# A negated-mean normalise on GpSimd and an earlier second-half projection in a layernorm, attention and mixture-of-experts kernel

## The reference

```python
xn = (x - mean(x)) / sqrt(var(x) + 1e-5)          # per token, over 128 features

# attention, per sequence of 256 tokens
w = einsum('bsd,btd->bst', xn @ W + b, xn)
w = exp(tanh(w * lw)) * off_diag                   # lw[s, t] = 1 / (|s - t| + 1e-7), 0 on the diagonal
attn = (w / (sum(w) + 1e-7)) @ xn

# mixture of 8 experts, top 2, 176 hidden units each, bf16 products
scores = sigmoid(xn @ gate_w.T)                    # top 2 of scores + expert_bias
routed = sum over the two of  square(relu((xn * score) @ w_up[e].T)) @ w_down[e].T

# shared expert, 176 hidden units, float32
shared = square(relu(xn @ shared_w_up.T)) @ shared_w_down.T

out = x + attn + routed + shared
```

## Time and profile before

| | |
|---|---|
| time, median of 3 runs | 118.33 us (117.22, 118.33 and 118.81) |
| span of the profiled execution, first to last instruction | 116.0 us |
| its own time, as the runs are timed | not given; the span lies 2.3 us below the median |
| busy: TensorE, its weight loads | 110.6 us, 85.1 us |
| busy: VectorE, ScalarE, GpSimd | 101.1 us, 89.5 us, 69.6 us |
| granted TensorE clock, mean of the span | 1.000 |

### The profile page before, as it was taken

One profiled execution on the slowest core, in us unless ns is written; L12 is line 12 of the kernel. 1 busy time (PEld: TensorE's weight loads), 2 busy tenths in 40 slices (PEclk: granted clock), 3 DMA queues, 4 the chain that ended last, 5 costly groups with the idle time before them and its releaser, 6 DMA issues.

```text
span 116.0 us, 2804 instructions
## 1 busy us (share of the span) xinstructions
PE 110.6 (95%) x914; PEld 85.1 (73%) x914; DVE 101.1 (87%) x319; ACT 89.5 (77%) x139; POOL 69.6 (60%) x119
## 2 busy tenths in 40 slices
PE   3988999999999999999999999999999999999991
PEld 3965558787868776869578776879588767859790
DVE  6969989999998989989998989988998689989751
ACT  4444799987788987969799687969699687897760
POOL 6538993499999499635973499636972520613200
PEclk9999999999999999999999999999999999999999
DMA  4999105886776759892849939593949648687882
GB/s 97 319 263 331 68 0 100 78 167 126 139 145 108 195 100 193 54 245 48 167 82 220 124 70 179 103 163 79 172 84 219 124 84 164 117 216 136 131 208 90
DMA packets 47965, 16.56 MB, mean 143 GB/s; under 512 B 45008, under 2 KB 45904, under 8 KB 47952
## 3 DMA queue, kind: packets, MB, share of 16 engines
q1 hardware_dynamic: 47376, 15.44, 66.0%
q0 software_dynamic: 288, 0.72, 3.2%
q10 hardware_dynamic: 288, 0.23, 1.0%
HBM read 3.84 MB, written 2.10 MB: 51 GB/s over the span
## 4 chain that ended last, share of the span: by engine, by line
PE 94%; DVE 1%; issue 1%; POOL 1%; ACT 0%; DVEq 0%; POOLq 0%
PE out_ps L1029 16%; PE h_ps L980 15%; PE side L957 12%; PE dots L936 11%; PE out_ps L1017 6%; PE out_ps L1011 4%; PE small L921 4%; PE side L970 4%; PE small L893 4%; PE out_ps L1059 4%; PE small L877 3%; PE h_ps L993 2%; PE small L902 1%; PE side L912 1%; PE side L921 1%
## 5 line engine op out<-in xcount | busy, mean ns | idle before, releaser
L698 DVE SCALAR_TENSOR_TENSOR gated<-h_ps,gates 128x1408 bf16<-128x1408 f32 x28 | 45.2, 1615 | 4.7 <-PE h_ps L980 4.4
L505 ACT ACTIVATE hidden<-gated 128x1408 bf16<-128x1408 bf16 x30 | 41.1, 1378 | 2.6 <-DVE gated L698 1.6
L1029 PE MATMUL out_ps<-downT,hiddenT 128*128 128x128 bf16 x341 | 22.8, 219 | 0.0
L1029 PEld LDWEIGHTS out_ps<-downT,hiddenT 128*128 128x128 bf16 x341 | 20.8, 98 | 2.3 <-issue 0.6
L980 PE MATMUL h_ps<-upT,xnTb 128*128 128x512 bf16 (+1 forms) x84 | 21.3, 362 | 0.0
L276 POOL TENSOR_SCALAR xn<-x_sb,meanvar,rstd 128x128 f32<-128x128 f32 x26 | 20.4, 795 | 0.6
L957 PEld LDWEIGHTS side<-xn,probs 128*128 128x128 f32 x120 | 15.1, 191 | 1.5 <-issue 0.5
L957 PE MATMUL side<-xn,probs 128*128 128x129 f32 x120 | 15.8, 274 | 0.0
L936 PE MATMUL dots<-projT,xnT 128*128 128x256 f32 x60 | 15.4, 379 | 0.0
L309 POOL TENSOR_SCALAR_AFFINE_SELECT probs<-probs 128x256 f32<-128x256 f32 x16 | 6.5, 408 | 12.7 <-ACT probs L462 12.6
L980 PEld LDWEIGHTS h_ps<-upT,xnTb 128*128 128x128 bf16 x84 | 7.2, 98 | 9.4 <-issue 3.2
(11 more groups left out here) (117 smaller groups left out, 178.9 us busy)
## 6 DMA issues: line engine op xcount, KB each, us to landing
x_sb<-in_x SPq DMA_DIRECT2D x7, 256.0 KB, 9.1
out_y<-final SPq DMA_DIRECT2D x7, 256.0 KB, 2.5
hiddenT<-hidden SPq DMA_TRANSPOSE x31, 3.6
upT<-in_up POOLq DMA_DIRECT2D x1, 352.0 KB, 7.5
downT<-in_down POOLq DMA_DIRECT2D x1, 352.0 KB, 8.4
late_sb<-in_late SPq DMA_DIRECT2D x1, 192.0 KB, 3.6
x_sb<-in_x ACTq DMA_DIRECT2D x1, 128.0 KB, 2.4
x_sb<-in_x SPq DMA_DIRECT2D x1, 128.0 KB, 2.5
```

The lines of the kernel that those rows point to most:

```text
L505: a.activation(hidden[:, t, :], gated[:, t, :], ACT.Square).then_inc(squared, 1)
L698: v.scalar_tensor_tensor(out=gated[:, t, :].rearrange("p (e h) -> p e h", e=E), in0=h_ps[:, 0:NH].rearrange("p (e h) -> p e h", e=E), scal ...
L1029: last = t_.matmul(out_at(c, t), hiddenT[:, c % 2, t, j, :], downT[:, j, :], start=(t == 0 and j == 0 and c < LAST), stop=((t >= 2 or c == ...
```

## The change

Three things are done. `rsqrt` gets one more GpSimd instruction, which writes the negated means of the four tiles into a new tile `neg_mean`, and its epsilon instruction gets a second operation, a product with 1.0. `normalize` adds `neg_mean` and multiplies by `rstd`, where it subtracted the mean and multiplied by `rstd`. (`normalize_fourth` on GpSimd and VectorE's two normalises stay as they are.) On TensorE `project_first(1)` goes from behind `dots(0, 0)` to behind `rest(0)`, ahead of `transpose_exp(0)`, and it waits in addition until ScalarE has read the first half out of the same bank.

```diff
+        neg_mean = sb("neg_mean", [P, 2, TILES])
...
             def rsqrt(c):
                 wait(pool, rstd_ready, c - 1)
                 pool.wait_ge(stats_ready, c + 1)
-                g.tensor_scalar(var_eps[:, :], meanvar[:, c % 2, :, 1], LN_EPS, None, ALU.add).then_inc(rstd_step, 1)
-                pool.wait_ge(rstd_step, c)
+                g.tensor_scalar(var_eps[:, :], meanvar[:, c % 2, :, 1], LN_EPS, 1.0, ALU.add, ALU.mult
+                                ).then_inc(rstd_step, 1)
+                g.tensor_scalar(neg_mean[:, c % 2, :], meanvar[:, c % 2, :, 0], -1.0, 0.0, ALU.mult, ALU.add
+                                ).then_inc(rstd_step, 1)
+                pool.wait_ge(rstd_step, 2 * c)
...
                 for t in range(at, to):
-                    g.tensor_scalar(xn[:, c, t, 0:D], x_sb[:, c, t, :], meanvar[:, c % 2, t, 0:1],
-                                    rstd[:, c % 2, t:t + 1], ALU.subtract, ALU.mult).then_inc(xn_ready, 1)
+                    g.tensor_scalar(xn[:, c, t, 0:D], x_sb[:, c, t, :], neg_mean[:, c % 2, t:t + 1],
+                                    rstd[:, c % 2, t:t + 1], ALU.add, ALU.mult).then_inc(xn_ready, 1)
...
             def project_first(half):
                 pe.wait_ge(early_loaded, 16)
                 if half:
                     pe.wait_ge(xT_taken, 1)
+                    pe.wait_ge(first_proj_taken, 1)
...
             rest(0)
+            project_first(1)
             transpose_exp(0)
             dots(0, 0)
-            project_first(1)
             up_tile(0, 0)
```

## The result

In the first comparison the changed kernel took 118.28 us (117.58 to 118.61, 14 runs) and the kernel before 117.8 us (117.02 to 118.81, 14 runs): a ratio of 1.0044, interval 1.0024 to 1.0065. Less than 2%, but slower, where I had forecast 0.07 us less. The ratios leave out runs that are over 1.5% above the fastest of the same kernel. The profiled execution after has a span of 116.4 us.

What follows compares the result with a forecast made beforehand. TensorE was taken to bound the steady loop, with GpSimd and VectorE leading at places in the start. A gain capped at 0.10 less 0.03 gave 0.07 us, so 118.3 us against a median of 118.33, range 117.2 to 119.0.

Steps and rivals of the forecast that it cites:

- Rival 1: GpSimd's normalise: add costs what subtract costs, so xn comes later in chunks 1 and 3; +0.3 to +0.4 us; chance 0.27.
- rival 2: TensorE's hole at the start is won in full, 0.43 us off the end, 117.9 us; chance 0.06.
- rival 4: GpSimd's new normalise form is much dearer, reaching 2% (2.4 us) at 1.1 us each; chance 0.03.
- rival 3: Moved projection starts the transposes of expneg 0.15 later, VectorE's run with them: +0.05 us, 118.4; chance 0.62 together with the forecast.
- The cap: At up_tile(0, 1): TensorE can win at most 0.10 us ahead of it unless VectorE's run from 10.09 to 14.66 changes.
- The 0.03 that I took off for VectorE: Transposes of expneg start 0.03 us later behind the moved projection, and VectorE's run to gate(0, 0) moves with them.
- from about 20 us TensorE is full: After gate and up_tile take turns from up_tile(0, 1) on, TensorE has no idle time left; no size given.
- Nothing in the steady loop adds to it: Steady loop: GpSimd waits for others and TensorE is full, so nothing is added to the 0.07 us gain.
- Part 1: Moved projection at the start: gains 0.40 us behind it, all spent waiting for xn of chunk 1 if that is unchanged.

Runs made afterwards that it cites:

- changed third: The changed kernel, not edited, third of its four profiled executions: first projection at 7.79, transfer 4.19 us, last down_tile at 112.50.
- before fourth: The kernel before, not edited, fourth of its four profiled executions: first projection at 7.79, transfer 4.16 us, last down_tile at 112.67.
- the one with 64 instructions: The changed kernel with sixteen tiny products on TensorE ahead of the warm-up: 117.51 us, ratio 0.9982.
- the last experiment on down_tile(0, 1): down_tile(0, 1) behind shared_down_rest(0): changed kernel 117.41 us, 0.9982; kernel before 117.85, 1.0003; changed kernel, behind transpose_exp(2) as well, 117.22, 0.9965.

## Why the prediction was wrong

**Right.** The normalise at 454 ns (0.48 taken from the rows of other operations; the row of the same form would have misled). The Trainium skill's rule ("GPSIMD Engine Reference", section 3.1), by which the estimate was about 0.30, is not borne out for add either. neg_mean at 0.20. xn of chunk 1 done at 10.24 + 0.95 = 11.19 in the first profile, and at 10.63 + 0.97 = 11.60 in the execution that starts as the kernel before did, against 11.55 predicted. VectorE's normalise_second is not held up. The wait for expneg is gone. At up_tile(0, 2) each edit alone is worth 0 to 0.06. The loop is as long as before: from up_tile(0, 2) to the last down_tile 112.50 - 17.28 = 95.22 us, against 112.67 - 17.46 = 95.21. Rival 1 (subtract's price for add), rival 2 (0.43 us won) and rival 4 did not occur. Nor did rival 3 by the path that it names: the transposes of expneg start 0.03 later (9.74 in changed third, 9.71 in before fourth), the size that I had taken, and not 0.15.

**Luck.** The forecast of 118.3 us agrees with the 118.28 measured, but it stands on 118.33, the median of three runs; by 14 runs the kernel before takes 117.8. The forecast was a gain of 0.07 and the first comparison a loss of 0.4%.

**Right in kind, too small.** I capped the gain at 0.10 less 0.03. Measured is 0.18. As predicted, up_tile(0, 1) waits for VectorE's gate(0, 0). Its weight loads, changed third and before fourth:

```profile
14.73 0.33 PEld L985 LDWEIGHTS h_ps<-upT,xnTb 128*128 128x128 bf16 x3 [0.85 <-DVE gated L702]
```

```profile
14.82 0.42 PEld L980 LDWEIGHTS h_ps<-upT,xnTb 128*128 128x128 bf16 x3 [0.56 <-DVE gated L698]
```

The loads lie 0.09 apart because the gate starts at 13.05 and 13.14, but that is not where the gain comes from: in the first profile of the kernel before the gate starts at 13.04 and the load at 14.72, as early as in the changed kernel, and up_tile(0, 2) is at 17.45 all the same. In both profiles of the kernel before the second matmul of up_tile(0, 1) comes at 15.13 to 15.14, behind the projection, and in changed third at 14.96. So the whole 0.18 is the projection that no longer streams there. The cap was too small by its term "A load takes 0.10 us, so at 14.82 it could have started", which is too long a time from a load to its matmul. The trace of before had a place without a projection in the way, up_tile(0, 2), and there the first matmul is 0.06 behind the start of its load:

```profile
17.39 0.38 PEld L980 LDWEIGHTS h_ps<-upT,xnTb 128*128 128x128 bf16 x3 [0.18 <-DVE gated L698]
```

```profile
17.45 0.76 PE L980 MATMUL h_ps<-upT,xnTb 128*128 128x512 bf16 x3
```

With 0.06 the cap would have been 0.14. The last 0.04 stands in no row: the first matmul of up_tile(0, 1) is missing from the trace of changed third. The 0.03 that I took off for VectorE did not reach it: gate(0, 0) is no later in the changed kernel.

**The step that failed** is the sentence "from about 20 us TensorE is full", with the sum's "Nothing in the steady loop adds to it". With it fails Part 1's "the part is worth nothing": the move alone took 118.72 us, ratio 1.0078. A TensorE without waits showed only that nothing was late in that execution, not by how much. At down_tile(0, 1) the transfer landed 0.05 us ahead of the load. I asked what would be late next once the stall is gone, and looked at GpSimd and VectorE, but not at the landing times of the DMAs that TensorE meets. That place is worth 1.0 us when the read falls badly, five times the change's gain, and it is no part of the code that the change touches. The kernel before has it as well.

**How often it falls badly, and what stays open.** The gain of 0.2 us is in every pair of profiles with the same start and the same place of the read, and the timed ratio of the changed kernel is nevertheless never under 1. The mean of the four ratios is 1.0020, or +0.24 us of 117.8. With -0.2 for the gain and 1.0 for a late transfer that needs the changed kernel to meet it in 0.44 more of its executions than the kernel before. The profiles lean that way: it was late in 2 of 4 against 1 of 4, and, counting the edited versions but the one with 64 instructions, in 8 of 10 executions with the new normalise against 2 of 7 with the old one; sorted by the move it is 8 of 10 and 2 of 7 as well. The profiles are few, but the times of all runs say the same. An execution without the late transfer took 117.75 us at the latest start (before fourth). Over 118.0 lie 29 of 50 runs of the changed kernel and 29 of 151 of the kernel before (two disturbed ones, of 145 and 165 us, left out), and none of the 36 runs of the three versions in the last experiment on down_tile(0, 1), which give the transfer more time. The line misses some of the changed kernel's late transfers: from an early start one takes it only to 117.81 us (its fourth profile). So 29 of 50 is a lower bound. So the change does make the late transfer more likely, and by the runs of one edit alone it is the move that does (6 of 7, against 3 of 12 for the normalise). The sorting is by time; only the profiled executions show the transfer itself.

No run shows why the move should shift the read. The changed kernel issues the second transfer 0.2 us later behind the first (17.24 to 20.12, against 17.62 to 20.30), which might lose a race that is decided within a few tenths; but the move alone has the distance of the kernel before (17.51 to 20.20) and is late all the same, and a later issue by half a microsecond did not win it back. What asks for the read at that moment was not found.

## What to carry to other kernels

Where one engine has no waits and so sets the time, list for each transfer that it meets when it lands and when the engine would load it: a margin of 0.05 us can be a wait in the next execution, and an early gain is spent there first. Before a difference of 0.4% is put down to an edit, profile both kernels several times, compare executions that begin alike, and look at how the times of single runs fall into groups: an occasional loss of 1 us shows there, not in a median. The one version under 1 puts two products with data at hand in front of the one with a thin margin (0.9965), while a longer move of three products cost about as much as it saved.

## What the runs showed of the hardware

- In chunks 0 and 1 a 16 KB read on the queue "instruction" goes with a longer time of the transposing transfer that it meets: 3.5 to 3.7 us without it, 3.9 to 4.2 when it comes within 0.7 us of the issue (which then takes 2.3 to 2.6 us instead of 1.39), and 5.0 to 5.3 when it comes later in the transfer. 64 more TensorE instructions ahead moved the read from 19.9 to 22.5 us (in the four executions of the unedited kernel) to 15.1; 16 more left it at 22.2.
- On GpSimd add and multiply by two per-partition columns took 454 ns for 128x128 float32, subtract and multiply 795 ns (the added column lies in a tile of its own).
- The first matmul behind a weight load that had waited started 0.06 us after its load did (17.39 and 17.45 before), where the load's own row is 0.10 us long.
- Executions of one program began their first projection between 7.04 and 7.79 us, as far apart as four times the change's gain.
